# Waits moved to where their data is used, four dummy activations for the table loads, and final waits on SyncE in a graph and mixture-of-experts kernel

## The reference, cut to what matters

```python
def _L0_gnn_ref(features, A, W1, b1, W2, b2):
    deg = jnp.sum(A, axis=0) + jnp.sum(A, axis=1) - jnp.diagonal(A)
    d_inv_sqrt = jnp.where(deg > 0, jax.lax.rsqrt(deg), 0.0)
    L_norm = d_inv_sqrt[:, None] * (jnp.diag(deg) - A) * d_inv_sqrt[None, :]
    _, U = jnp.linalg.eigh(L_norm)                      # 64 x 64
    agg = jnp.einsum('mn,bnd->bmd', U.T, features)
    return jnp.einsum('nm,bmd->bnd', U, jax.nn.relu(agg @ W1 + b1) @ W2 + b2)
...
x = x + _L0_gnn_ref(_layernorm(x), adj, ...)   # eigenvectors of the graph
x = x + _L0_ffn_ref(_layernorm(x), ...)        # 8 experts with Gelu, the best 2 of each token
x = x + _L1_gnn_ref(_layernorm(x), adj, ...)   # two graph layers, then LSTMs over 1 to 4 steps
x = x + _L1_ffn_ref(_layernorm(x), ...)        # Gelu layer, gate, 8 experts, the best 1 of each token
```

## Time and profile before

| | |
|---|---|
| time, median of 3 runs | 1480.25 us (1479.82 to 1482.68) |
| span of the profiled execution | 1478.8 us |
| PE busy | 1131.6 us, 77% of the span |
| PEld busy | 828.3 us, 56% |
| DVE busy | 829.8 us, 56% |
| ACT busy | 761.6 us, 52% |
| POOL busy | 558.1 us, 38% |
| mean granted TensorE clock | 0.900 of full speed |

### The profile page before, as it was taken

The page is one execution under the profiler, slowest core; times in us unless marked ns, Lnnn a source line. Parts: engine busy times, 40 slices in busy tenths (PEclk is TensorE's granted clock), DMA queues, the critical chain, the costliest instruction groups (busy, mean ns, idle before and its releaser), DMA issues. The chain is left out here.

```text
span 1478.8 us, 28089 instructions
## 1 busy us (share of the span) xinstructions
PE 1131.6 (77%) x6361; PEld 828.3 (56%) x6362; DVE 829.8 (56%) x3890; ACT 761.6 (52%) x2089; POOL 558.1 (38%) x855
## 2 busy tenths in 40 slices
PE   2444422628771999999958998999999789929995
PEld 1223321527661999999955554445544345419995
DVE  4777799986774333345547773444444568622221
ACT  3555543614430666666636775665555456505552
POOL 3666614800467772054537500000000005654553
PEclk9999965669865999999978999999999889959998
DMA  9400000000012332233312100000000002233330
GB/s 261 130 1 1 1 1 0 2 0 5 29 46 72 108 121 89 68 108 106 105 54 53 40 5 0 0 0 0 0 0 0 4 1 76 84 129 109 105 105 26
DMA packets 85702, 75.59 MB, mean 51 GB/s; under 512 B 13206, under 2 KB 74847, under 8 KB 85612
## 3 DMA queue, kind: packets, MB, share of 16 engines
q1 hardware_dynamic: 71788, 44.64, 10.9%
q0 software_dynamic: 13824, 29.98, 6.4%
HBM read 41.72 MB, written 33.37 MB: 51 GB/s over the span
## 5 line engine op out<-in xcount | busy, mean ns | idle before, releaser
L1207 POOL DMA_INDIRECT z<-spent,seats x64 | 63.1, 986 | 401.6 <-DVE spent L1328 383.9
L1673 ACT ACTIVATE c_H<-ps,c_b 128x128 f32<-128x128 f32 x576 | 156.8, 383 | 96.8 <-PE ps L1719 96.8
L2218 PE MATMUL ps<-BIG,spent 128*128 x364 | 156.1, 578 | 3.3 <-ACTq L2231 3.3
L1719 PE MATMUL ps<-ZS,c_w 128*128 128x128 f32 x1152 | 142.5, 277 | 3.4 <-ACT ZS L1662 2.2
L1705 PE MATMUL ps<-spent,c_H 128*128 x1152 | 140.3, 275 | 0.0
L1719 PEld LDWEIGHTS ps<-ZS,c_w 128*128 128x128 f32 x1152 | 136.0, 194 | 4.5 <-ACT ZS L1662 3.0
L1705 PEld LDWEIGHTS ps<-spent,c_H 128*128 128x128 f32 x1152 | 134.3, 192 | 0.0
L2218 PEld LDWEIGHTS ps<-BIG,spent 128*128 128x128 f32 x364 | 69.7, 192 | 84.6 <-issue 84.6
L2226 PE MATMUL ps<-e_hs,spent 128*128 128x512 f32 (+1 forms) x256 | 110.0, 572 | 0.0
L856 POOL DMA_INDIRECT z<-BIG,spots x64 | 62.9, 983 | 111.7 <-DVE spots L973 94.4
L1573 POOL DMA_INDIRECT c_rows<-y,seats x64 | 60.5, 946 | 114.0 <-DMA y<-c_ys 59.4
(11 more groups left out here) (507 smaller groups left out, 2669.5 us busy)
## 6 DMA issues: line engine op xcount, KB each, us to landing
BIG<-z SPq DMA_DIRECT2D x72, 129.0 KB, 2.0
ZB<-z SPq DMA_DIRECT2D x144, 64.0 KB
y<-c_ys SPq DMA_DIRECT2D x72, 128.0 KB
spent<-in_L_ffn_W_dram SPq DMA_DIRECT2D x1, 2048.0 KB
spent<-in_L_ffn_W_dram SPq DMA_DIRECT2D x8, 256.0 KB
w_dn<-in_L_ffn_Wd_dram SPq DMA_DIRECT2D x8, 256.0 KB
z<-BIG,spots POOLq DMA_INDIRECT x128, 2.2
z<-j_padding SPq DMA_DIRECT2D x9, 129.0 KB, 2.9
```

Of the source, the lines that this page charges most:

```text
L1207: pool.indirect_dma_start(z, bass.IndirectOffsetOnAxis(ap=k.seats[:, 0, n:n + 1], axis=0), k.R[:, row(n), :], None, bounds_check=E * STRID ...
L1673: act.activation(H[u][:, c, h * P:(h + 1) * P], UP[u][c // 2][:, o:o + P], ACT.Gelu, bias=b1[u][h][:, c:c + 1]).then_inc(gelu, 1)
L1719: pe.matmul(UP[u][c // 2][:, o:o + P], w1[u][h][:, c * P:(c + 1) * P], ZT[u][:, h * P:(h + 1) * P], start=True, stop=True).then_inc(up, 1)
L2218: last = pe.matmul(view(k.ps[4 * u + j], wide, lanes), k.w_ihT[:, w, :], state(i, u, s, p, wide, lanes), start=True, stop=(s == 0))
```

## The change

- **Constants.** POOL makes the identity right after the two zeroed tiles; the other constants follow.
- **Transposes.** PE no longer waits for all constants ahead of the transpose of A, and makes a second one of the left half of A alone, to `ps[3]`. DVE reads that for A + A', instead of waiting for ACT's copies.
- **DVE's constants** of L494 to L504 stand ahead of A + A' and wait for the identity only. `s_matrix` is incremented by M itself. The copy to L0 stands after x.
- **ACT's order.** The Sqrt to `root` stands ahead of `adjsum`.
- **Loads.** Each quarter of X has its semaphore, awaited ahead of the first tile of the quarter. POOL awaits and adds the bias rows in step 12 (ROWS_AT).
- **Dummy activations** on one column, into a new tile `warm`: Sqrt at the start, Gelu after the Exp of gate 0, Sigmoid at the start of the graph layers, Gelu at the start of the last gate.
- **End.** The eight waits for `placed[b]` stand on SP instead of POOL.

```diff
--- before
+++ after
@@ -61,2 +61,3 @@
 AT_ROOT = GROUPS - 1
+ROWS_AT = 12
 DEPTH = 8
...
@@ -174,2 +175,3 @@
+        s_x = [sem(f"h_x{q}") for q in range(4)]
         ch, s_load = k.ch, k.s_load
@@ -183,3 +185,3 @@
                 r = slice(q * TILES // 4, (q + 1) * TILES // 4)
-                sp.dma_start(k.X[:, r, :], x_tok[:, r, :]).then_inc(s_x, 16)
+                sp.dma_start(k.X[:, r, :], x_tok[:, r, :]).then_inc(s_x[q], 16)
             for dst, src in loads["rows"](rows, rows2):
@@ -197,2 +199,5 @@
             pool.memset(pivot[:, :], 0.0).then_inc(s_pool, 1)
+            pool.wait_ge(s_pool, 2)
+            pool.affine_select(out=ident[:, :], in_=ident[:, :], compare_op=ALU.not_equal, fill=1.0, base=0,
+                               pattern=[[-1, P]], channel_multiplier=1).then_inc(s_pool, 1)
             consts = [pool.memset(ones[:, :], 1.0), pool.memset(BDU[:, :], 0.0), pool.memset(BDUT[:, :], 0.0), pool.memset(BDAT[:, :], 0.0),
@@ -205,5 +210,2 @@
                 ins.then_inc(s_const, 1)
-            pool.wait_ge(s_pool, 2)
-            pool.affine_select(out=ident[:, :], in_=ident[:, :], compare_op=ALU.not_equal, fill=1.0, base=0,
-                               pattern=[[-1, P]], channel_multiplier=1).then_inc(s_pool, 1)
             pool.memset(pivot[:, N:N + 1], 1.0).then_inc(s_const, 1)
@@ -213,6 +215,7 @@
                                pattern=[[-1, P]], channel_multiplier=1).then_inc(s_const, 1)
-            pool.wait_ge(s_pool, 3)
-            pool.wait_ge(s_rows, 16 * 5)
-            pool.tensor_tensor(rows[0:SKIPS * GATES, :], rows[0:SKIPS * GATES, :], rows2[:, :], ALU.add).then_inc(s_sum, 1)
             for i in range(STEPS):
+                if i == ROWS_AT:
+                    pool.wait_ge(s_rows, 16 * 5)
+                    pool.tensor_tensor(rows[0:SKIPS * GATES, :], rows[0:SKIPS * GATES, :], rows2[:, :],
+                                       ALU.add).then_inc(s_sum, 1)
                 pool.wait_ge(s_row, i + 1)
@@ -258,3 +261,4 @@
         def _(act):
-
+            act.wait_ge(s_pool, 2)
+            act.activation(k.warm[:, :], pivot[:, 0:1], ACT.Sqrt)
             act.wait_ge(s_turned, 1)
@@ -263,2 +267,4 @@
             act.activation(BDAT[N:P, N:P], ps[0][N:P, 0:N], ACT.Copy).then_inc(s_turned_sb, 1)
+            act.wait_ge(s_square, 1)
+            act.activation(root[:, :], half_B[:, :], ACT.Sqrt).then_inc(s_rooted, 1)
             act.wait_ge(s_rowsum, 1)
@@ -266,4 +272,2 @@
                            ps[6][0:1, None, 0:N].to_broadcast([1, GC // N, N]), ACT.Copy).then_inc(s_turned_sb, 1)
-            act.wait_ge(s_square, 1)
-            act.activation(root[:, :], half_B[:, :], ACT.Sqrt).then_inc(s_rooted, 1)
             def unused(n):
@@ -272,2 +276,4 @@
             def token_mean(n):
+                if n % (TILES // 4) == 0:
+                    act.wait_ge(s_x[n // (TILES // 4)], 16)
                 if n >= 2 * GT:
@@ -282,3 +288,2 @@
 
-            act.wait_ge(s_x, 16 * 4)
             for i in range(STEPS):
@@ -365,4 +370,5 @@
             pe.wait_ge(s_pool, 3)
-            pe.wait_ge(s_const, CONSTS)
             pe.transpose(ps[0][:, 0:N], A[:, :], ident[0:N, 0:N]).then_inc(s_turned, 1)
+            pe.transpose(ps[3][0:N, 0:N], A[:, 0:N], ident[0:N, 0:N]).then_inc(s_turned, 1)
+            pe.wait_ge(s_const, CONSTS)
             pe.wait_ge(s_offd, 1)
@@ -469,5 +475,16 @@
 
-            dve.wait_ge(s_turned_sb, 2)
-            dve.wait_ge(s_const, CONSTS)
-            link(tt_(junk[0:N, :], A[:, 0:N], ps[0][0:N, 0:N], ALU.add))
+            dve.wait_ge(s_pool, 3)
+            link.put(dve.memset(nudge, NUDGE))
+            link.put(dve.memset(OFF[:, :], 0.0))
+            link.put(ts_(minus[:, :], ident[:, 0:N], -1.0, None, ALU.mult))
+            for r, o in ((slice(0, N), slice(N, P)), (slice(N, P), slice(0, N))):
+                link.put(dve.tensor_copy(swap[:, r], ident[:, o]))
+                link.put(tt_(both[:, r], ident[:, r], ident[:, o], ALU.add))
+            link.put(dve.memset(upper_half[:, N:P], 0.0))
+            link(dve.memset(lower_half[:, 0:N], 0.0))
+            link.put(dve.tensor_copy(upper_half[:, 0:N], both[:, 0:N]))
+            link.put(dve.tensor_copy(lower_half[:, N:P], both[:, N:P]))
+            link.put(dve.tensor_copy(M[:, N:P], ident[0:N, 0:N]))
+            dve.wait_ge(s_turned, 2)
+            link(tt_(junk[0:N, :], A[:, 0:N], ps[3][0:N, 0:N], ALU.add))
             link(tt_(offd[:, :], A[:, 0:N], ident[0:N, 0:N], ALU.mult))
@@ -491,15 +508,3 @@
             link(stt(out=half_B[0:N, :], in0=junk[0:N, :], scalar=-0.5, in1=half_B[0:N, :], op0=ALU.mult, op1=ALU.add))
-            link(tt_(M[:, 0:N], half_B[0:N, :], scale[0:N, :], ALU.mult))
-            link(dve.tensor_copy(L0[:, :], M[:, 0:N]))
-            link(dve.memset(nudge, NUDGE))
-            link(dve.memset(OFF[:, :], 0.0))
-            link(ts_(minus[:, :], ident[:, 0:N], -1.0, None, ALU.mult))
-            for r, o in ((slice(0, N), slice(N, P)), (slice(N, P), slice(0, N))):
-                link.put(dve.tensor_copy(swap[:, r], ident[:, o]))
-                link.put(tt_(both[:, r], ident[:, r], ident[:, o], ALU.add))
-            link.put(dve.memset(upper_half[:, N:P], 0.0))
-            link(dve.memset(lower_half[:, 0:N], 0.0))
-            link.put(dve.tensor_copy(upper_half[:, 0:N], both[:, 0:N]))
-            link(dve.tensor_copy(lower_half[:, N:P], both[:, N:P]))
-            dve.tensor_copy(M[:, N:P], ident[0:N, 0:N]).then_inc(s_matrix, 1)
+            tt_(M[:, 0:N], half_B[0:N, :], scale[0:N, :], ALU.mult).then_inc(s_matrix, 1)
             dve.wait_ge(s_xm, 1)
@@ -508,2 +513,3 @@
             dot(dve, junk_x[:, 1:N], x[:, 1:N], ident[:, 1:N], xc).then_inc(s_xcol, 1)
+            link.put(dve.tensor_copy(L0[:, :], M[:, 0:N]))
             link.reset()
@@ -1083,2 +1089,3 @@
         act.activation(ex[:, :], ex[:, :], ACT.Exp).then_inc(s_exd, 1)
+        act.activation(k.warm[:, :], k.prio[:, 0:1], ACT.Gelu)
 
@@ -1809,2 +1817,4 @@
         rounds(sp, fetch, NT, DEPTH + 4, 0)
+        for b in range(DEPTH):
+            sp.wait_ge(placed[b], 16 * HALVES * len(range(b, NT, DEPTH)))
 
@@ -1818,4 +1828,2 @@
                                         ).then_inc(placed[b], 16)
-        for b in range(DEPTH):
-            pool.wait_ge(placed[b], 16 * HALVES * len(range(b, NT, DEPTH)))
 
@@ -2092,2 +2100,3 @@
 
+            act.activation(k.warm[:, :], k.prio[:, 0:1], ACT.Sigmoid)
             normalized(0, range(GT))
@@ -2346,2 +2355,3 @@
         k.prio = sb("prio", [P, E])
+        k.warm = sb("warm", [P, 1])
         k.LG = sb("LG", [P, TILES, E])
```

More of the change, by code:

```diff
@@ L165, in spectrum @@
         raw = [k.BIG[:, u * 2048:(u + 1) * 2048].rearrange("q (w d) -> q w d", d=P) for u in range(2)]
-        (s_adj, s_rows, s_raw, s_x, s_const, s_pool, s_turned, s_turned_sb, s_offd, s_deg, s_square, s_rooted,
+        (s_adj, s_rows, s_raw, s_const, s_pool, s_turned, s_turned_sb, s_offd, s_deg, s_square, s_rooted,
          s_matrix, s_row, s_length, s_inverse, s_ycol, s_half, s_sign, s_xs, s_xcol, s_beta, s_q, s_ntyc, s_scaled, s_xm, s_ym, s_mean, s_var, s_scale,
@@ L170, in spectrum @@
          s_ritz_row, s_factor, s_refined) = (sem("h_" + n) for n in (
-             "adj rows raw x const pool turned turned_sb offd deg square rooted matrix row length inverse "
+             "adj rows raw const pool turned turned_sb offd deg square rooted matrix row length inverse "
              "ycol half sign xs xcol beta q ntyc scaled xm ym mean var scale std z za tokens tokens_sb zw zw_sb diag diag_row "
@@ L365, in _ @@
             pe.wait_ge(s_pool, 3)
+            pe.transpose(ps[0][:, 0:N], A[:, :], ident[0:N, 0:N]).then_inc(s_turned, 1)
+            pe.transpose(ps[3][0:N, 0:N], A[:, 0:N], ident[0:N, 0:N]).then_inc(s_turned, 1)
             pe.wait_ge(s_const, CONSTS)
-            pe.transpose(ps[0][:, 0:N], A[:, :], ident[0:N, 0:N]).then_inc(s_turned, 1)
             pe.wait_ge(s_offd, 1)
```

## The result

The changed kernel took 1475.96 us in the median of seven runs (1470.52 to 1478.35), the kernel before beside it 1482.46 (1479.82 to 1486.47): a ratio of 0.9948, interval 0.9932 to 0.9965. Once more, in a later session (e4), it was 0.9943 (0.9931 to 0.9955). It is faster by 0.3 to 0.7%; the medians are 6.5 us apart in the first session and 9.6 in the second. Forecast were 1465.5, range 1462.5 to 1470.5: the direction was right, the size was not.

A forecast was written before the change was run, and what follows sets the result against it. The prediction took the kernel as one core's chain of stages, so gains ahead of step 0 move all the rest. Terms −9.3 − 0.55 − 0.9 + 1.4 − 5.4 = −14.75 took 1480.25 to 1465.5 us, range 1462.5 to 1470.5.

The forecast's parts named there:

- Start: Ahead of and in the first reflection step: first Square 8.2 us earlier, step 0 1.1 shorter; 9.3 gained, bounds 8.2 to 9.6.
- Step 0: First reflection step: 4.11 us before because POOL came late; with POOL ready 2.8 to 3.1, a gain of 1.1.
- Gelu: Ahead of the first experts: a dummy removes the 1.28 us table load; 0.55 us gained, between 0 and 1.28.
- Sigmoid: Ahead of the first graph stage: a dummy removes the table load at 789.17; 0.9 us gained, between 0.5 and 1.28.
- Last gate: Gelu dummy at the last gate's start: its load has no cover, costing 1.4 us, between 0 and 1.5.
- End: Final waits moved to SP: POOL's DRAIN ends 5.3 us behind the last scatter, as two earlier DRAINs did; 5.4 us gained.
- The bound, 1.6: At the end: a DRAIN behind scatters takes its 9.19 us whenever it starts, so only 1.6 us gained.
- The base and the middle: Starting time 1480.25 us, 1.4 above the profiled span, taken as unchanged; middle stages keep their lengths within a microsecond or two.
- if the middle stages don't keep their lengths within a microsecond or two: Stated sign of a wrong prediction; loads misplaced or a slower clock there eating 2 to 6 us, 1467 to 1472, had 0.07.
- The rival on the clock: First experts fall to 1.2 GHz; 3 us slower than before needs 35 us more of it; at or above before, 0.02.
- the DRAIN's rival: At the end: POOL's DRAIN keeps its 9.2 us, 1.6 gained instead of 5.4, time 1469.3 us; chance 0.22.
- The rule of 12 ns: At the end: with DRAINs that short, the last edit gives nothing, 1470.9 us; not on the path, 0.02.

The follow-up runs named there:

- e4: The changed kernel once more, nothing altered, on the same chip as the parts: 1476.08 us, ratio 0.9943.
- e2: The kernel before with only its final eight waits moved from POOL to SP: 1484.01 us, ratio 0.9985.
- e7: The changed kernel with its last block's 72 output scatters on POOL replaced by plain DMAs of SP, rows in another order: 1478.71 us, one run.
- e11: The changed kernel without the last gate's Gelu dummy, with 11 and 4 extra matmuls in the graph layers, 27 and 24 ahead of the experts: 1467.49 us.
- e6: The changed kernel without the last gate's Gelu dummy, with extra matmuls: 13 starting the graph layers, 16 and 14 ahead of the experts: 1473.85 us.
- e5: The changed kernel with 13 extra matmuls ahead of PE's first wait in the graph layers: 1475.42 us.
- e9: The changed kernel with only the first 18 of 36 tiles scattered by POOL, the others written by SP to scratch: 1468.5 us, one run.

## Why the prediction was wrong, step by step

- **Start**, −9.3: measured −9.8 on the first block's end in the first profile, −9.6 in e4; by the line through the runs −8.9. Right, the first a little past its bound of 9.6. Step 0 took 2.68 us (11.25 to 13.93), less than the 2.8 to 3.1 forecast. Nothing I took as covered came up: not DVE's set-up, not X.
- **Gelu**, −0.55: −0.3 to −0.6 in the two profiles. Right.
- **Sigmoid**, −0.9: 154.7 to 153.8 in e4. Right where the block is short; among the long ones there is no difference (158.7 in e2 without, 158.7 with it), as ACT is not what is late there.
- **Last gate**, +1.4: 1.36 where it stands, about 1 at the block's end; the line through the runs has 1.7 to 2.6, with errors of 0.8 each. Right by the traces.
- **End**, −5.4: −1.5. This is the term that was mis-sized. "I take the first, as the nearer in what is queued, though those two follow gathers and not scatters": being queued was not what makes a DRAIN short, and neither was following gathers (e7). The DRAIN ended 9.2 us behind the last scatter and not 5.3. What the move saves is POOL's wait for the landings alone. The bound, 1.6, was the answer, and with it the sum was −11.0, against −11.1 measured between two traces with short blocks. That the two agree so closely is in part luck, with the last gate 0.6 better and gate 0 0.6 worse than forecast.
- **The base and the middle.** "The profiled execution spans 1478.8, the median of the three runs is 1480.25": both were near the quick end of the kernel before. Of its 43 runs in this study the median is 1485.2 and four are at or below 1481. A difference of 11 us taken off a favourable run gives a favourable run of the changed kernel (1469.6 in e4), not its median. The forecast named what would break it, "if the middle stages don't keep their lengths within a microsecond or two", and gave it 7 in 100. The rival on the clock put a fall into the first experts and asked "35 us more"; what happened is some 8 and 10 us more at 0.5 in gate 0 and the graph layers (an estimate: 2 × (1 − clock) × length, from the rows before and after, whose clocks are rounded), in the graph layers at a place where PE was waited for, and the blocks grew by 2.8 and 4.0 us, the latter by 4.9 against e4. It happens in the kernel before as well (e2).

So of the miss of 10.5 us, 3.9 are the DRAIN. Another 3.9 are the clock, by the line's 0.98 us: the base was read at 0.900, and the changed kernel's seven runs have 0.896 in the median. The other 2.7 us are no larger than the errors of the line's levels together, and are assigned to nothing. With the DRAIN's rival alone, 1469.3, the forecast would still have been 6.7 us short.

The rule of 12 ns for the DRAINs of the preamble and postamble (the Trainium skill, "VectorE: DVE Perf Modes", "The DRAIN you can't avoid") can't be carried over to POOL's DRAIN at a block's end: behind indirect DMAs that took 5.3 us and more in every run here. The 1380 ns added to a table load (the Trainium skill, "ScalarE: Activation LUTs", "What ACT_TABLE_LOAD costs") would have made the last dummy cost 2.7 us, an estimate; PE's first wait grew by 1.36, and the measurement decides.

## What to carry to other kernels

Before a forecast is made against a profiled run, see where that run lies among the others, and compare its granted clock: a run 5 us below the median takes 5 us off every result. Where TensorE's clock falls in an idle stretch, matmuls that nobody reads can hold it up. Here they helped only where they reached up to the first real product (e11) and not where they ended some 10 us ahead of it (e6), and they move a block only if that product is what is waited for. A duration is not to be carried from one block's DRAIN to another's when its cause is not known: the bound from this block's own row was the answer.

## What was not expected of the hardware

- The granted clock of TensorE came back at different moments of the same program, run by run, and gave blocks of two lengths, 4.9 us apart in the graph layers. The line through the runs is 0.98 us for each 0.001 of mean clock, yet in e5 the graph layers were 4.8 us longer at a higher mean clock, since the half clock lay in the wrong place.
- POOL's last DRAIN took 5.3 us with no scatter of output rows ahead of it in its block, ended 8.2 us behind the last DMA with 36, whether they ended just ahead of the end or 60 us earlier, and 9.2 with 72: a cost that can be paid while other engines work if POOL's DMAs end early (e9).
